# Leaving out 38 TensorE transposes of the identity ahead of the first gate product

## Chip, cores and metric

The kernel runs on one core of a Trainium2 chip. The metric is the device time of one execution in microseconds (us). The time of before is the median of three executions. One more execution was profiled; all rows below are from it. Engines: PE is TensorE, with its weight loads (PEld) recorded apart from its matmuls; DVE is VectorE, ACT ScalarE, POOL GpSimd, SP SyncE.

## The reference, cut to what matters

Two layers on `x` of shape (4, 256, 256): four batches `b`, 256 tokens, 256 channels. Each layer first makes its input by a bidirectional recurrence over tokens, gated by `sigmoid(x)`, and feeds it to a feed-forward part, whose output is added to `x`:

```python
x = x + _L0_ffn_ref(_L0_cond_ref(x, F, F, L0_w, L0_u, cond), A, Bw, Wg)
x = x + _L1_ffn_ref(_L1_cond_ref(x, F, F, L1_w, L1_u, cond), w1, b1, w2, b2)

def _bi_wkv(r, k, v, w, u, time_emb):      # both cond parts
    a = a * decay + exp(k) * v             # forward scan: num; with exp(k) alone: den
    ...                                    # the same backward
    return sigmoid(r) * (num / den) * (0.8 + 0.2 * tf)

def _L0_ffn_ref(x, A, Bw, Wg):             # top-1 mixture of 8 experts, rank 64
    prob = softmax(x @ Wg.T); gate = argmax(prob)
    h = einsum('nd,erd->ner', x, A) * one_hot(gate)
    return einsum('ner,eor->no', h, Bw) * 4 * prob[gate]

def _L1_ffn_ref(x, w1, b1, w2, b2):        # 256 -> 1024 -> 256, gelu, ternary weights
    return gelu(x @ q(w1).T + b1) @ q(w2).T + b2
```

The transposes that the change leaves out write a part of PSUM that nothing reads. They are no part of what is computed.

## The kernel before, in words

Channels lie on the 128 partitions (two halves `c`), tokens on the free axis, so that VectorE can do each recurrence as a scan along tokens. All engines have their instructions written out by hand, in one list for each, and wait for each other only by semaphores. TensorE's list is strictly in order: a wait in it holds back all that is listed behind it.

The work goes layer by layer and batch by batch, interleaved. For a batch of the first layer: VectorE scans forward (L708) and backward (L726), numerator and denominator; ScalarE takes logarithm and exponential for a reciprocal; VectorE or GpSimd multiply; `ratio` on VectorE (L738) ends this and raises `ratio_ready`. Then TensorE makes the gate product `gate_logits` (L1023: 8 columns, eight matmul records, each with the load of a 128x128 f32 weight) and the two halves of the first expert product, `expert_in` (L1038, sixteen records of 256 columns). VectorE reads the logits (`gate`, L743 to L755), makes the mask of the chosen expert (`expert_mask`, L768), TensorE transposes it (`transpose_mask`, L1045), ScalarE copies it out of PSUM (`copy_mask`, L473), VectorE multiplies it into the expert product (`select_expert`, L776), and TensorE makes the second expert product (`expert_out`, L1054). After that come tanh and the second layer, whose two products are `hidden` (L1101) and `ffn_out` (L1134).

The change touches TensorE's list alone. What stands in it just ahead of the gate product of batch 0 is `place_residual` (L1009), then `weight_totals` (L1062), which waits for ScalarE's sum over the second weight matrix (L497), and then five calls of `keep_warm`. Each waits for `AT_ready` and for one step of VectorE's (or GpSimd's) work on the first ratios, and then transposes the 128x128 identity `ident` (made at the start, and constant) into bank 7, 6, 8, 8, 8 and 8 times: 38 transposes (L939). The steps are the forward and backward numerator scans of batches 0 and 1, and `dr_ready[0]`, raised by `den_times_rec` (L236) just ahead of `ratio(0, 0)`. Bank 7 held a transposed half of A, which `AT_ready` says has been copied out. `warm_up(8)`, at the very start of the list (L933), stays.

After the gate product of batch 0 the list goes on:

```python
            gate_logits(0)
            expert_in(0, 0)
            expert_in(0, 1)
            transpose_mask(0)
            transpose_weights(0)
            gate_logits(1)
            expert_in(1, 1)
            expert_out(0)
```

VectorE's list at this place is `ratio(0, 0)`, `thresholds` (L781, L783), `backward(0, 2, DEN)`, `gate(0)`, `gate_index(0)`, `own_keys(0, 3)`, `times_sigmoid(1)`, `expert_mask(0)`, `ratio(0, 1)`, `own_values(0, 2)` (L216), `select_expert(0, 1)`, `select_expert(0, 0)`, `gate(1)`. ScalarE's is `sign_below(0)`, `gate_exp(0)`, `sign_above(0)`, `copy_mask(0)`, `sign_above(1)`.

Of the kernel before, what the change touches and what calls it, by code (L numbers as in the profile page):

```python
# [14 lines left out]
P = 128  # L15
# [8 lines left out]
def adaln_ffn_kernel(nc, x, fside, cond, w_l0, u_l0, A, Bw, Wg, w_l1, u_l1, w1, b1, w2, b2, out):  # L24
# [6 lines left out]
    NE, R, _ = A.shape  # L31
# [14 lines left out]
    with ExitStack() as ctx:  # L46
        def sb(name, shape, dt=F32, where=ctx):
            return where.enter_context(nc.sbuf_tensor(name, shape, dt))

        def sem(name):  # L50
            return ctx.enter_context(nc.semaphore(name))

        bank = [ctx.enter_context(nc.psum_tensor(f"bank{k}", [P, 512], F32)) for k in range(8)]

        ident = sb("ident", [P, P])
# [72 lines left out]
        def per(kind, n):  # L128
            return [sem(f"{kind}_{k}") for k in range(n)]
# [16 lines left out]
        fwd_done, seeded, bwd_done = [[per(f"{kind}{q}", RING) for q in ("num", "den")] for kind in ("fwd_", "seed_", "bwd_")]  # L146
        den_ready, num_ready = per("den_ready", RING), per("num_ready", RING)
        ln_done, rec_ready = per("ln_done", RING), per("rec_ready", RING)
        dr_ready, q_ready, ratio_ready = per("dr_ready", RING), per("q_ready", RING), per("ratio_ready", RING)
        qsig_ready = per("qsig_ready", NB)  # L150
        Wg_psum, A_psum, B_psum = sem("Wg_psum"), sem("A_psum"), sem("B_psum")
        WgT_ready, AT_ready, BT_ready = sem("WgT_ready"), sem("AT_ready"), sem("BT_ready")
# [18 lines left out]
        COND_BANK, DECAY_BANK, WARM_BANK, WT_BANK, MISC_BANK = 4, 5, 7, 4, 6  # L171
# [7 lines left out]
        NUM, DEN = 0, 1  # L179
# [748 lines left out]
        def _(pe):  # L928
# [3 lines left out]
                for _ in range(n):  # L932
                    pe.transpose(bank[WARM_BANK][:, 0:P], ident[:, :], ident[:, :])  # L933

            def keep_warm(done, count, n):
                pe.wait_ge(AT_ready, 2)
                pe.wait_ge(done, count)
                for _ in range(n):
                    pe.transpose(bank[WARM_BANK][:, 0:P], ident[:, :], ident[:, :])  # L939

            def transpose_vectors():
                pe.wait_ge(vec_loaded, 16 * 4)
                pe.transpose(bank[MISC_BANK][:, VEC_AT:VEC_AT + NV], vec_rows[:, :], ident[0:NV, 0:NV]).then_inc(vec_psum, 1)
# [68 lines left out]
            def gate_logits(b):  # L1012
                r, u = ring(0, b)
                pe.wait_ge(ratio_ready[r], u + 1)
                if b == 0:
                    pe.wait_ge(WgT_ready, 2)
                else:
                    pe.wait_ge(logits_ready, b)
                    pe.wait_ge(mask_copied, b)
                for n in range(NT):  # L1020
                    at = LOGIT_AT + NE * n
                    for c in range(NC):
                        mm = pe.matmul(bank[MISC_BANK][:, at:at + NE], nd[:, r, c, NUM, n * P:(n + 1) * P], WgT[:, c],  # L1023
                                       start=(c == 0), stop=(c == NC - 1))
                mm.then_inc(logits_psum, 1)
# [32 lines left out]
            def weight_totals():  # L1058
                pe.wait_ge(wsum_ready, 2)
                pe.wait_ge(consts_ready, 3)  # L1060
                pe.wait_ge(BT_ready, 2)
                pe.matmul(bank[WT_BANK][:, 0:2], ones[:, :], wsum[:, :], start=True, stop=True).then_inc(wtot_psum, 1)  # L1062
# [95 lines left out]
            place_residual(0)  # L1158
            place_residual(1)
            weight_totals()  # L1160
            keep_warm(fwd_done[NUM][0], 2, 6)
            keep_warm(bwd_done[NUM][0], 2, 8)
            keep_warm(fwd_done[NUM][1], 2, 8)
            keep_warm(bwd_done[NUM][1], 2, 8)
            keep_warm(dr_ready[0], 1, 8)
            gate_logits(0)
            expert_in(0, 0)
            expert_in(0, 1)
# [104 lines left out]
```

## Time and profile before

| | |
|---|---|
| median of three executions | 126.23 us (126.23, 126.23, 126.68) |
| profiled execution, its own time | 126.34 us |
| its span, first to last instruction | 124.5 us |
| around the span | 1.84 us |
| granted TensorE clock, mean over the span | 0.918 |
| busy share of the span | PE 81%, PEld 75%, DVE 87%, ACT 67%, POOL 42% |

Matmul and weight-load records overlap each other, so a group's busy time is less than its count times its mean duration; the pace of a group is read from the starts of its records. In the view by windows each column after the window and its length is an engine's busy time in it, with the number of records in brackets.

### The profile page before, as it was taken

What the parts mean: (1) busy time and instruction counts of PE and PEld (TensorE: products, weight loads), DVE (VectorE), ACT (ScalarE), POOL (GpSimd) and SP (SyncE); (2) the same over time, 40 slices, a digit from 0 to 9 for tenths busy, and PEclk for the clock granted to TensorE, in tenths of its full rate; (3) what the DMA queues carried; (4) which work ended last, traced back from release to release, by engine and by line L of the source; (5) the groups of instructions that cost most, each with busy time, mean ns of one, the idle gap of its engine ahead of it and who ended that gap; (6) DMA issues with size and microseconds to landing.
All of it is one profiled execution on the core that took longest, in us unless ns stands there. A gap on an engine that the chain in (4) does not pass through costs nothing.

```text
span 124.5 us, 2082 instructions
## 1 busy us (share of the span) xinstructions
PE 101.1 (81%) x654; PEld 93.7 (75%) x654; DVE 108.2 (87%) x218; ACT 83.0 (67%) x148; POOL 51.7 (42%) x61
## 2 busy tenths in 40 slices
PE   5596791099987999699725999967989799989991
PEld 5485790099976889599524899956979799989990
DVE  1389999999999999999999997999999999994731
ACT  4186989940676934469248549878099996997441
POOL 3077484817071149095703528409440390000530
PEclk9999689756999599999985599999999999999999
DMA  3899990000000000000000000000000002020004
GB/s 91 278 311 304 309 382 13 0 8 0 0 0 0 0 0 3 5 3 0 0 0 3 0 0 0 5 0 0 0 0 5 0 0 84 0 87 5 0 3 168
DMA packets 7271, 6.44 MB, mean 52 GB/s; under 512 B 2370, under 2 KB 7004, under 8 KB 7260
## 3 DMA queue, kind: packets, MB, share of 16 engines
q1 hardware_dynamic: 7244, 6.31, 16.3%
q8 instruction: 5, 0.08, 0.3%
q14 instruction: 6, 0.05, 0.1%
q10 hardware_dynamic: 16, 0.00, 0.0%
HBM read 5.26 MB, written 1.05 MB: 51 GB/s over the span
## 4 chain that ended last, share of the span: by engine, by line
DVE 58%; PE 17%; issue 17%; DMA 2%; DVEq 1%; ACT 1%; ACTq 0%
DVE run L708 14%; DVE nd L726 11%; PE bank L1134 6%; DVE own L695 4%; PE bank L1054 4%; DVE hm L776 4%; DVE mask L768 3%; PE bank L1101 3%; DVE nd L738 3%; DVE run L716 2%; DMA vec_rows<-in_L_cond_u_dram 2%; DVE nd L250 2%; DVE h_lo L262 2%; DVE nd L236 2%; DVE nd L223 2%
## 5 line engine op out<-in xcount | busy, mean ns | idle before, releaser
L708 DVE TENSOR_TENSOR_SCAN run<-bank,kv 128x256 f32<-128x256 f32 x32 | 20.1, 669 | 0.4
L726 DVE TENSOR_TENSOR_SCAN nd<-bank,run 128x256 f32<-128x256 f32 x32 | 20.1, 673 | 0.2
L1054 PE MATMUL bank<-hm,BT 128*128 128x256 f32 x64 | 16.9, 423 | 1.5 <-DVE hm L776 1.5
L1038 PE MATMUL bank<-nd,AT 128*128 128x256 f32 x64 | 17.7, 431 | 0.0
L1101 PE MATMUL bank<-xin_hi,w1T 128*128 128x256 f32 x64 | 15.8, 287 | 1.7 <-ACT h L536 1.2
L1054 PEld LDWEIGHTS bank<-hm,BT 128*128 128x128 f32 x64 | 13.6, 217 | 4.2 <-DVE hm L776 1.9
L262 POOL TENSOR_TENSOR h_lo<-h,h_hi 128x512 fp32r<-128x512 f32 x6 | 8.1, 1348 | 20.4 <-DVE h_hi L270 14.0
L1134 PE MATMUL bank<-w2T,h_hi 128*128 128x256 f32 x64 | 15.9, 287 | 0.5 <-DVE h_lo L262 0.5
L1038 PEld LDWEIGHTS bank<-nd,AT 128*128 128x128 f32 x64 | 15.8, 330 | 0.4
L1134 PE MATMUL bank<-w2T,h_lo 128*128 128x256 f32 x64 | 15.3, 278 | 0.0
L1101 PE MATMUL bank<-xin_lo,w1T 128*128 128x256 f32 x64 | 15.2, 279 | 0.0
L536 ACT ACTIVATE h<-bank,bT 128x256 f32<-128x256 f32 x32 | 12.9, 474 | 2.8 <-PE bank L1101 2.8
L1101 PEld LDWEIGHTS bank<-xin_hi,w1T 128*128 128x128 f32 x64 | 12.1, 189 | 2.2 <-issue 1.6
L1134 PEld LDWEIGHTS bank<-w2T,h_hi 128*128 128x128 f32 x64 | 12.0, 188 | 0.8 <-DVE h_lo L262 0.7
L216 POOL TENSOR_TENSOR own<-own,vs 128x512 f32<-128x512 f32 x6 | 8.2, 1361 | 9.9 <-DVE own L695 7.8
L1101 PEld LDWEIGHTS bank<-xin_lo,w1T 128*128 128x128 f32 x64 | 12.1, 189 | 0.0
L1134 PEld LDWEIGHTS bank<-w2T,h_lo 128*128 128x128 f32 x64 | 12.0, 188 | 0.0
L236 POOL TENSOR_TENSOR nd<-nd,run 128x512 f32<-128x512 f32 x5 | 6.4, 1272 | 12.2 <-ACT run L457 12.2
L230 POOL TENSOR_TENSOR nd<-nd,own 128x512 f32<-128x512 f32 x5 | 6.7, 1335 | 9.7 <-DVE nd L726 9.7
L262 DVE TENSOR_TENSOR h_lo<-h,h_hi 128x512 fp32r<-128x512 f32 x10 | 8.0, 796 | 2.0 <-ACT h_hi L269 1.9
L452 ACT ACTIVATE run<-nd 128x512 f32<-128x512 f32 x8 | 5.0, 623 | 6.1 <-DVE nd L223 6.1
L716 DVE TENSOR_TENSOR run<-run,inv_gain 128x2 f32<-128x2 f32 x16 | 7.6, 477 | 1.0
(131 smaller groups left out, 236.5 us busy)
## 6 DMA issues: line engine op xcount, KB each, us to landing
w_nat<-in_L_ffn_w_dram SPq DMA_DIRECT2D x2, 1024.0 KB, 8.1
F_nat<-in_fside_BxSxS_dram SPq DMA_DIRECT2D x4, 256.0 KB, 4.1
x_nat<-in_x_dram SPq DMA_DIRECT2D x4, 256.0 KB, 5.0
out_dram<-outb SPq DMA_DIRECT2D x3, 256.0 KB, 2.1
A_nat<-in_L_ffn_A_dram SPq DMA_DIRECT2D x1, 512.0 KB, 5.7
B_nat<-in_L_ffn_Bw_dram SPq DMA_DIRECT2D x2, 256.0 KB, 6.7
out_dram<-outb SPq DMA_DIRECT2D x2, 128.0 KB, 1.7
vec_rows<-in_L_cond_w_dram ACTq DMA_DIRECT2D x2, 1.0 KB
```

What stands on the lines that cost most here:

```text
L216: eng.tensor_tensor(own[:, r, :, NUM, :], own[:, r, :, DEN, :], vs[:, b], ALU.mult).then_inc(ownv_ready[r], 1)
L230: eng.tensor_tensor(num, num, own[:, r, :, NUM, :], ALU.add).then_inc(num_ready[r], 1)
L236: eng.tensor_tensor(den, den, run[:, r, :, DEN, :], ALU.mult).then_inc(dr_ready[r], 1)
L262: eng.tensor_tensor(h_lo[:, b % 2, 2 * j:2 * j + 2], h32[:, 2 * j:2 * j + 2], h_hi[:, b % 2, 2 * j:2 * j + 2].bitcast(F32), ALU.subtract). ...
L536: act.activation(h32[:, f], bank[g_bank[NJ * b + j]][:, (f % 2) * T:(f % 2 + 1) * T], ACT.Gelu, bias=bT[:, f:f + 1], scale=0.5).then_inc(h ...
L708: dve.tensor_tensor_scan(run[:, r, c, q], decay_ps[:, l, c, b:b + 1].broadcast_to([P, T]), kv[:, b, c, q], 0.0, ALU.mult, ALU.add).then_in ...
L716: dve.tensor_tensor(last, last, inv_gain[:, l, :, b], ALU.mult).then_inc(seeded[q][r], 1)
L726: dve.tensor_tensor_scan(nd[:, r, c, q, ::-1], decay_ps[:, l, c, b:b + 1].broadcast_to([P, T]), run[:, r, c, q, ::-1], 0.0, ALU.mult, ALU. ...
L1038: mm = pe.matmul(bank[H_BANK + k][:, (m % 2) * T:(m % 2 + 1) * T], AT[:, c, m::NM], nd[:, r, c, NUM, :], start=(c == 0), stop=(c == NC - 1))
L1054: mm = pe.matmul(bank[y_bank[b % 2]][:, o * T:(o + 1) * T], BT[:, m, o * P:(o + 1) * P], hm[:, b % 2, m], start=False, stop=(o == NC - 1 a ...
L1101: mm = pe.matmul(bank[g_bank[g]][:, (f % 2) * T:(f % 2 + 1) * T], w1T[:, c, f * P:(f + 1) * P], part[:, b % 2, c], start=(c == 0 and part ...
L1134: mm = pe.matmul(o_region(b, n), part[:, b % 2, f, n * P:(n + 1) * P], w2T[:, f], start=False, stop=(f == NF - 1 and part is h_lo and (n = ...
```

## The change

`keep_warm` and its five calls are taken out: 38 transposes on TensorE, with the waits ahead of them. No other engine's list changes, and no wait of any other instruction names anything that these transposes signal, for they signal nothing.

```diff
-            def keep_warm(done, count, n):
-                pe.wait_ge(AT_ready, 2)
-                pe.wait_ge(done, count)
-                for _ in range(n):
-                    pe.transpose(bank[WARM_BANK][:, 0:P], ident[:, :], ident[:, :])
-
...
             place_residual(0)
             place_residual(1)
             weight_totals()
-            keep_warm(fwd_done[NUM][0], 2, 6)
-            keep_warm(bwd_done[NUM][0], 2, 8)
-            keep_warm(fwd_done[NUM][1], 2, 8)
-            keep_warm(bwd_done[NUM][1], 2, 8)
-            keep_warm(dr_ready[0], 1, 8)
             gate_logits(0)
             expert_in(0, 0)
             expert_in(0, 1)
```

## Rows read from the trace of the kernel before

**Rows 1.** The page: the granted clock in 40 slices, and the chain by engine
```profile
PEclk9999689756999599999985599999999999999999
...
DVE 58%; PE 17%; issue 17%; DMA 2%; DVEq 1%; ACT 1%; ACTq 0%
```

**Rows 2.** Timeline of the weight loads: start us, length us, line, tiles, count, idle before
```profile
24.89 0.50 PEld L1062 LDWEIGHTS bank<-wsum,ones 128*128 128x128 f32 x2 [6.05 <-ACT h L497]
25.13 6.78 PEld L939 LDWEIGHTS bank<-ident 128*128 128x128 f32 x38
31.88 0.97 PEld L1023 LDWEIGHTS bank<-WgT,nd 128*128 128x128 f32 x8
32.77 3.83 PEld L1038 LDWEIGHTS bank<-nd,AT 128*128 128x128 f32 x16
38.08 0.20 PEld L1045 LDWEIGHTS bank<-ident,mask 128*128 128x128 f32 x2 [1.48 <-DVE mask L768]
```

**Rows 3.** Windows: length, busy PE, PEld, DVE, ACT, POOL, granted clock, DMA
```profile
16.50:17.00 0.50, 0.50 (x6) 0.50 (x5) 0.40 (x2) 0.25 (x1) 0.50 (x2) 0.74 1.05 416
...
19.03:23.58 4.55, 0.00 (x0) 0.00 (x0) 4.47 (x10) 4.51 (x7) 2.55 (x3) 1.00 0.00 1
23.58:24.89 1.31, 0.00 (x0) 0.00 (x0) 1.31 (x2) 1.26 (x2) 1.26 (x1) 0.50 0.00 0
25.34:30.41 5.07, 5.07 (x25) 5.07 (x26) 4.97 (x7) 1.35 (x2) 3.00 (x2) 0.50 0.01 3
30.41:31.88 1.47, 1.47 (x16) 1.47 (x14) 1.32 (x4) 0.00 (x0) 0.01 (x1) 1.00 0.00 0
40.65:44.06 3.41, 3.41 (x10) 2.71 (x10) 3.21 (x13) 3.17 (x9) 1.01 (x1) 0.50 0.00 0
67.88:71.37 3.49, 3.49 (x8) 2.86 (x9) 3.28 (x7) 2.36 (x3) 1.41 (x2) 0.50 0.00 0
```

**Rows 4.** Timeline of VectorE around the first gate
```profile
31.08 0.69 DVE L738 SCALAR_TENSOR_TENSOR nd<-nd 128x512 f32<-128x512 f32 x1
31.95 1.26 DVE L726 TENSOR_TENSOR_SCAN nd<-bank,run 128x256 f32<-128x256 f32 x2
33.13 0.15 DVE L743 COPY logits<-bank 128x16 f32<-128x16 f32 x1
35.80 2.23 DVE L768 TENSOR_SCALAR mask<-expert_of,idx,grec 128x128 f32<-128x128 f32 x2
39.15 1.28 DVE L776 TENSOR_TENSOR hm<-bank,mask_rows 128x512 f32<-128x512 f32 x2
```

**Rows 5.** Timeline of PE: weight totals and the first gate product
```profile
24.89 0.59 PE L1062 MATMUL bank<-wsum,ones 128*128 128x2 f32 x2 [5.86 <-ACT h L497]
31.99 0.96 PE L1023 MATMUL bank<-WgT,nd 128*128 128x8 f32 x8
```

**Rows 6.** Timeline of PEld: A's and B's transposes; `expert_out(2)` at each clock
```profile
13.16 0.59 PEld L969 LDWEIGHTS bank<-ident,x_nat 128*128 128x128 f32 x4 [1.97 <-issue]
13.74 1.72 PEld L986 LDWEIGHTS bank<-ident,A_nat 128*128 128x128 f32 x8
15.44 1.61 PEld L995 LDWEIGHTS bank<-ident,B_nat 128*128 128x128 f32 x8
68.05 0.76 PEld L1054 LDWEIGHTS bank<-hm,BT 128*128 128x128 f32 x2
70.60 0.76 PEld L1054 LDWEIGHTS bank<-hm,BT 128*128 128x128 f32 x2
```

**Rows 7.** Timeline of ScalarE: the mask's copy
```profile
38.56 0.38 ACT L473 ACTIVATE mask_rows<-bank 128x256 f32<-128x256 f32 x1 [2.01 <-PE bank L1045]
```

**Rows 8.** Timeline of PE and VectorE, 57 to 76 us: waits around `expert_out(2)`
```profile
57.97 3.67 PE L1054 MATMUL bank<-hm,BT 128*128 128x256 f32 x16
67.88 5.43 PE L1054 MATMUL bank<-hm,BT 128*128 128x256 f32 x16 [0.69 <-DVE hm L776]
75.53 0.17 DVE L743 COPY logits<-bank 128x16 f32<-128x16 f32 x1 [0.55 <-PE bank L1023]
```

## The prediction

> **What bounds the kernel now.** I read the page first: the chain that ended last is VectorE for 58% of the span, TensorE for 17% [rows 1]. The removed transposes lie in a stretch where VectorE is the chain, so they matter in two ways only: if the gate product had to queue behind them, and by what they do to TensorE's clock, which the slices show at half speed in four places [rows 1].
>
> The timeline of weight loads comes next [rows 2]. TensorE sat idle for 6.05 us until ScalarE's sum released `weight_totals` at 24.89. All 38 transposes then ran without a gap from 25.13 to 31.88, because most of their waits were over before they began. The gate product's loads started at 31.88, with the last transpose's load just ended. `ratio(0, 0)` ended at 31.08 + 0.69 = 31.77 [rows 4]. So the gate product followed its true releaser by 0.11 us.
>
> The windows show the clock [rows 3]. It was at 1.2 GHz (0.50) from 23.58, after 4.55 us without one TensorE record, through the first 25 transposes, and rose to 2.4 GHz (1.00) at 30.41, with nothing but transposes and the two small products of `weight_totals` behind it. The gate product and the first expert product ran at 2.4 GHz. TensorE then waited for VectorE: the mask's loads sat idle for 1.48 us before 38.08 [rows 2].
>
> **What the change does, step by step.**
>
> *The place in the queue.* The gate product's first load can start as soon as `ratio(0, 0)` releases it. The mask ended at 35.80 + 2.23 = 38.03 and its transpose's load began at 38.08 [rows 2, 4]: 0.05 us from end to start. So the load comes at 31.82 instead of 31.88 and 0.05 us (rounded down) is gained. Nothing else waited for the transposes.
>
> *The clock when the gate product starts.* TensorE now has nothing from about 25.4 to 31.82, some 6.4 us. The clock is low at 25.4 already; after an idle stretch of 4.55 us it was taken away, not given [rows 3]. So it stays at 1.2 GHz at 31.82.
>
> *The gate product at 1.2 GHz.* It is bound by its loads of 128x128 f32 weights: eight from 31.88 to 32.77, 0.111 us each [rows 2]. Loads of the same shape at 1.2 GHz ran at (15.44 - 13.74) / 8 = 0.2125 us [rows 6]. So the eight take 1.70 us instead of 0.89, and the expert product's first load comes at 31.82 + 1.70 = 33.52. The last gate matmul ends behind that load's start: by 31.99 + 0.96 - 32.77 = 0.18 us before [rows 2, 5]; at 1.2 GHz by 24.89 + 0.59 - 25.13 = 0.35 us (`weight_totals`, the next load at 25.13) [rows 2, 5]. It ends at 33.87, and with 0.05 us to the release VectorE's copy starts at 33.92 instead of 33.13 [rows 4]. The wait was hidden before: VectorE came to the copy from its own scan (31.95 + 1.26) [rows 4]. Now it is bare, **+0.8 us** on VectorE's list, and nothing in that list can go ahead of it. What hangs on it moves along: `own_keys(0, 3)`, on which GpSimd waits, `gate_exp` on ScalarE, and the mask, now released at 38.08 + 0.8 = 38.9.
>
> *The first expert product.* Its sixteen loads took 3.83 us at 2.4 GHz, 0.24 each [rows 2]. At 1.2 GHz the same form (`expert_out(2)`) had seven starts, that is six steps, from 68.05 to 70.60: 0.425 us each [rows 6]. What counts is when the clock rises. From restart to rise it took 71.37 - 67.88 = 3.5 us, 16.76 - 13.16 = 3.6 us (0.74 in the window 16.50:17.00 puts the rise at 16.76), and 30.41 - 24.89 = 5.5 us [rows 2, 3, 6]. From 31.82 these give 35.3 to 37.3; counted from the expert product at 33.52, since the gate product moves few columns, 37.0 to 39.0. I take 37.1, where the two readings meet. By then 8.4 loads have gone at 0.425; the other 7.6 take 1.8 us and end at 38.9. That is the moment when the mask is ready. So the 1.48 us in which TensorE waited is used up, and nothing is added. With a rise at 35.3 the mask is last, also nothing; with one at 39.0 the loads end at 33.52 + 12.9 x 0.425 + 3.1 x 0.24 = 39.75; with none, at 33.52 + 16 x 0.425 = 40.3. The mask's copy ended at 38.56 + 0.38 = 38.94 and its reader began at 39.15 [rows 4, 7], so 0.2 us more is free. The delay there is 0.8 us for an early or middle rise, 39.75 - 38.08 - 0.2 = 1.5 us for a late one and 2.2 us for none. I take 0.8, and keep 1.5 for the range.
>
> *Up to about 68 us.* TensorE's low stretch from 40.65 to 44.06 [rows 3] may go, as TensorE no longer idles just before it. I cost that at nothing: VectorE is the chain there, and its next wait for TensorE is at 75.53 [rows 8]. So the 0.8 us is carried on.
>
> *From 68 to 76 us.* `expert_out(2)` is on the chain, took 5.43 us (3.67 for `expert_out(1)` at 2.4 GHz) and was at 1.2 GHz until 71.37 [rows 3, 8]. Starting 0.8 us later, it gains nothing if the rise also comes 0.8 us later, and 0.8 x (1 - 0.24 / 0.425) = 0.35 us if it stays at 71.37, because less of it is then slow. The three distances from restart to rise differ by 2 us, so the trace favours neither end: I take the middle, **-0.15 us**. More than 0.55 us can't come back here, since VectorE waited just that long for TensorE [rows 8].
>
> **Sum**, against the profiled execution: 126.34 + 0.8 - 0.15 = 127.0 us (the queue's 0.05 is in the 0.8). It stood 0.11 above the median, which gives 126.9.
>
> **The rivals.**
>
> *The clock returns late.* The gate product may not count toward the rise and the next rise come 5.5 us after 33.52, or not before the expert product ends: delay 1.5 to 2.2 us, 127.6 to 128.3. For it: the 5.5 us of the restart at 24.89. Against it: dense products brought the clock back in 3.5 us at 67.88 [rows 3].
>
> *Not slower: the debt is paid back at `expert_out(2)`.* Its place is 67.88 to 75.53. Run wholly at 2.4 GHz it would be 5.43 - 3.67 = 1.76 us shorter, of which the 0.55 us that VectorE waits are on the chain. The time is 126.23 + 0.8 - 0.55 = 126.5, no change that can be told. It decides once the rise comes at least 0.55 / (1 - 0.24 / 0.425) = 1.3 us earlier, counted from the product's start, than the 3.49 us of before, or if the clock never falls near 64 us, because the preceding product, now 0.8 us later, fills what was idle. For it: that stretch moves toward the fall. Against it: TensorE still has a gap there of several us, with a few bf16 products in it.
>
> *The transposes do nothing for the clock.* Then before's rise at 30.41 had another cause, the gate product runs at 2.4 GHz in either kernel, and the 0.05 us is all: 126.2. Against it stands the rise itself [rows 3]. The Trainium skill ("TensorE: Matmul & The Clock Gate", part 4, on transposes by TensorE) says that full clock "doesn't engage" for transposes, as they don't count as busy in the same way; by that page the change would cost nothing. The trace disagrees: 38 transposes lay behind the change at 30.41.
>
> *Faster by over 0.5%.* For this the delay must stay away and the clock be higher at `expert_out(2)` as well; 126.23 - 0.05 - 0.55 = 125.6.
>
> **How the numbers follow.** 0.5% (0.63 us, a bound at 126.86) is about what a measurement of this kernel can tell from no change; its three executions spread by 0.45. Forecast 0.58: within it the delay at the end lies between 0.45 and 0.9 us, 126.6 to 127.1, with 0.37 of it above the bound and 0.21 below. Late clock 0.14, slower. Paid back 0.17, same. No effect 0.06, same. Faster 0.05. So slower 0.51, same 0.44, faster 0.05. For the range I leave out what lies below 126.3 (most of no effect, and faster) and the upper half of the late clock: 126.3 to 127.8.
>
> **What would show it right or wrong.** Right: no TensorE record between about 25.5 and 31.8; granted clock 0.50 there and through the gate product; its loads 0.21 us apart; VectorE's copy of the logits at about 33.9 with a wait of about 0.7 us for TensorE ahead of it; the mask's loads idle for almost nothing; the same distances between VectorE's steps from there to 68 us. Wrong: a granted clock of 1.00 at 31.9 (then the rule on transposes holds); a rise later than 38 us and a second wait of VectorE at its multiplication by the mask; a VectorE wait at the fourth gate's copy well away from 0.55 us; or a last-ended chain that no longer goes through VectorE between 33 and 68 us.

## The result and the profile after

Over nine executions each, the changed kernel took 127.77 us (127.14 to 128.44) and the kernel before 126.41 us (126.23 to 126.81): ratio 1.0108, 95% interval 1.008 to 1.0136. It is slower by about 1.4 us. The forecast of 126.9 had the sign and half of the size; the measured time lies 0.03 us inside the upper end of its range, 127.8. Ratios, here and below, are over the executions within 1.5% of the fastest of their kernel and medians over all, and where almost none lies that near the fastest only the median is given.

The profiled execution took 127.68 us, its span 125.8.

From here on, times inside an execution are also given from the start of `ratio(0, 0)`, since the first small loads land earlier or later by up to half a microsecond from one execution to the next and move all that follows; a plus sign marks such a time. That start is 31.08 before [rows 4] and 30.52 after.

The page of the changed kernel, clock in 40 slices and chain by engine:

```profile
PEclk9999689755569999968997569999999999999999
...
DVE 50%; PE 28%; issue 14%; ACT 2%; DMA 2%; DVEq 1%; ACTq 0%
```

TensorE's share of the chain rose from 17% [rows 1] to 28%, though it has 38 transposes less. The half-speed slices lie elsewhere: on through 31 to 37 us, a new place near 54 to 58, and near 68 to 75. The chain went through TensorE's gate product and first expert product from 31.27 to 38.8, where before it was VectorE's, and then, behind the copy of the mask, through VectorE up to the multiplications by the mask of batch 2 at 67.9.

Timeline of its weight loads, first gate to first mask (the lines are six lower than before):

```profile
31.27 1.78 PEld L1017 LDWEIGHTS bank<-WgT,nd 128*128 128x128 f32 x8 [6.34 <-DVE nd L738]
32.93 5.58 PEld L1032 LDWEIGHTS bank<-nd,AT 128*128 128x128 f32 x16
38.42 0.38 PEld L1039 LDWEIGHTS bank<-ident,mask 128*128 128x128 f32 x2
```

Timeline of its VectorE, at the same places as [rows 4, 8], and the mask of batch 2:

```profile
30.52 0.69 DVE L738 SCALAR_TENSOR_TENSOR nd<-nd 128x512 f32<-128x512 f32 x1
...
33.19 0.17 DVE L743 COPY logits<-bank 128x16 f32<-128x16 f32 x1 [0.53 <-PE bank L1017]
...
35.87 2.23 DVE L768 TENSOR_SCALAR mask<-expert_of,idx,grec 128x128 f32<-128x128 f32 x2
...
39.55 1.29 DVE L776 TENSOR_TENSOR hm<-bank,mask_rows 128x512 f32<-128x512 f32 x2 [0.25 <-ACT mask_rows L473]
...
61.28 2.66 DVE L768 TENSOR_SCALAR mask<-expert_of,idx,grec 128x128 f32<-128x128 f32 x2 [0.20 <-DVE grec L761]
...
77.82 0.17 DVE L743 COPY logits<-bank 128x16 f32<-128x16 f32 x1 [1.52 <-PE bank L1017]
```

The gate product's eight loads took 1.66 us (32.93 - 31.27) instead of 0.89. The copy of the logits came 2.67 us after `ratio(0, 0)` began, before 2.05: **0.62 us late**. The sixteen loads of the expert product took 5.5 us instead of 3.8 (38.42 - 32.93) and ended behind the mask (35.87 + 2.23 = 38.10), and the first multiplication by the mask began at +9.03 instead of +8.07: **0.96 us late**, with a wait for ScalarE's copy that was not there before. Then the delay was carried unchanged until the mask of batch 2, which took 2.66 us instead of 1.74. Windows show where the clock was (columns as in [rows 3]):

```profile
36.50:37.00 0.50, 0.50 (x3) 0.35 (x2) 0.50 (x2) 0.00 (x0) 0.50 (x2) 0.50 0.00 0
37.00:37.50 0.50, 0.50 (x4) 0.50 (x3) 0.50 (x1) 0.00 (x0) 0.50 (x1) 0.89 0.00 0
50.60:52.60 2.00, 0.15 (x3) 0.00 (x0) 2.00 (x5) 0.60 (x1) 0.00 (x0) 1.00 0.00 0
54.20:57.50 3.30, 3.30 (x8) 2.68 (x9) 3.20 (x11) 3.19 (x3) 2.88 (x3) 0.50 0.01 2
67.90:74.60 6.70, 5.73 (x17) 4.39 (x15) 6.39 (x11) 3.18 (x5) 2.53 (x3) 0.50 0.00 1
```

The rise came at 37.11 (0.89 of the window from 37.00). A new low stretch lies over the expert product of batch 2, at 54.2 to 57.5, some 1.5 us after the end of a pause of TensorE (0.15 us busy in 50.60 to 52.60).

How that reached VectorE is seen on ScalarE and GpSimd. The kernel before, timelines of the three engines at batch 2:

```profile
58.78 0.57 ACT L517 ACTIVATE w2T<-bank 128x512 fp32r<-128x512 f32 x1
59.26 0.70 ACT L457 ACTIVATE run<-run,recip_bias 128x512 f32<-128x512 f32 x1
...
60.04 1.27 POOL L236 TENSOR_TENSOR nd<-nd,run 128x512 f32<-128x512 f32 x1 [0.76 <-ACT run L457]
61.26 1.27 POOL L243 TENSOR_TENSOR nd<-nd,run 128x512 f32<-128x512 f32 x1
...
60.87 1.74 DVE L768 TENSOR_SCALAR mask<-expert_of,idx,grec 128x128 f32<-128x128 f32 x2 [0.21 <-DVE grec L761]
```

The changed kernel at the same place:

```profile
60.08 0.60 ACT L517 ACTIVATE w2T<-bank 128x512 fp32r<-128x512 f32 x1 [0.80 <-PE bank L1073]
60.58 0.71 ACT L457 ACTIVATE run<-run,recip_bias 128x512 f32<-128x512 f32 x1
...
61.37 1.27 POOL L236 TENSOR_TENSOR nd<-nd,run 128x512 f32<-128x512 f32 x1 [1.67 <-ACT run L457]
62.59 1.26 POOL L243 TENSOR_TENSOR nd<-nd,run 128x512 f32<-128x512 f32 x1
```

The slow expert product made TensorE's weight transposes behind it late. ScalarE waited 0.80 us for them in `evacuate_wT(4)`, which copies them out of PSUM (L517). `reciprocal(1, 0)` (L457) stood behind it in ScalarE's list, and so GpSimd's two products that need the reciprocal (the pair, L236 and L243) came 0.92 us later against the start of the mask's instructions (61.37 - 61.28 against 60.04 - 60.87). VectorE's second mask instruction ended only when that pair had: mask end 63.94, pair end 63.85 (before: 62.61 and 62.53). Where the pair misses them, the two instructions take 0.60 us. So the mask lost 0.92 us more than before. `expert_out(2)` was at 1.2 GHz almost throughout and VectorE waited 1.52 us at the fourth gate (that of batch 3) instead of 0.55; of the 2.85 us that it was late there, 1.2 were given back by the next mask (82.49, +51.97, before 81.37, +50.29), since two of VectorE's small steps no longer met GpSimd. At VectorE's last copy it stood at +92.65 against +90.82: 1.83 us late, about as much as the 0.96 at the first multiplication and the 0.92 at this mask together.

### The profile page after: what moved, and what is told of

It reads as the page before. It is cut to its first block, busy times and chain, and to the rows that moved or that the text cites. A ratio compares the mean times of both kernels' runs of the same rounds, so it can differ in the third digit from the quotient of the medians.

```text
span 125.8 us, 2001 instructions
## 1 busy us (share of the span) xinstructions
PE 97.9 (78%) x616; PEld 89.6 (71%) x616; DVE 108.0 (86%) x218; ACT 83.0 (66%) x148; POOL 51.8 (41%) x61
## 4 chain that ended last, share of the span: by engine, by line
DVE 50%; PE 28%; issue 14%; ACT 2%; DMA 2%; DVEq 1%; ACTq 0%
DVE run L708 12%; DVE nd L726 10%; PE bank L1032 8%; PE bank L1128 6%; PE bank L1048 5%; PE bank L1095 4%; DVE own L695 4%; DVE hm L776 4%; DVE nd L738 3%; DVE mask L768 2%; DVE run L716 2%; PE bank L1017 2%; DMA vec_rows<-in_L_cond_u_dram 2%; DVE h_lo L262 2%; DVE nd L236 2%
## 5 line engine op out<-in xcount | busy, mean ns | idle before, releaser
L1032 PE MATMUL bank<-nd,AT 128*128 128x256 f32 x64 | 19.7, 470 | 0.0
L1048 PE MATMUL bank<-hm,BT 128*128 128x256 f32 x64 | 17.4, 433 | 1.2 <-DVE hm L776 1.2
L1032 PEld LDWEIGHTS bank<-nd,AT 128*128 128x128 f32 x64 | 17.1, 330 | 1.5
L236 POOL TENSOR_TENSOR nd<-nd,run 128x512 f32<-128x512 f32 x5 | 6.3, 1270 | 14.6 <-ACT run L457 14.6
L1017 PE MATMUL bank<-WgT,nd 128*128 128x8 f32 x32 | 5.0, 282 | 8.3 <-DVE nd L738 8.2
L1017 PEld LDWEIGHTS bank<-WgT,nd 128*128 128x128 f32 x32 | 4.7, 225 | 8.7 <-DVE nd L738 8.4
L509 ACT ACTIVATE below<-w_nat,thr 128x2048 bf16<-128x2048 f32 x2 | 4.0, 2002 | 7.6 <-DVE thr L783 4.7
```

The lines of the kernel that those rows point to most:

```text
L236: eng.tensor_tensor(den, den, run[:, r, :, DEN, :], ALU.mult).then_inc(dr_ready[r], 1)
L1032: mm = pe.matmul(bank[H_BANK + k][:, (m % 2) * T:(m % 2 + 1) * T], AT[:, c, m::NM], nd[:, r, c, NUM, :], start=(c == 0), stop=(c == NC - 1))
L1048: mm = pe.matmul(bank[y_bank[b % 2]][:, o * T:(o + 1) * T], BT[:, m, o * P:(o + 1) * P], hm[:, b % 2, m], start=False, stop=(o == NC - 1 a ...
```

## The experiments

Ratios are against the kernel before on the same chip. "Before" had a median of 126.5 to 126.6 us in these calls and spread from 125.1 to 127.7 over more executions than were seen at first.

**The delay alone, at full clock** (`late_gate`; the kernel before, edited; `fill(n)` is n transposes of `ident` into bank 7 without a wait):

```diff
+            pe.wait_ge(ratio_ready[0], 1)
+            fill(7)
             gate_logits(0)
```

> The kernel before, with seven more transposes of the identity put between the end of ratio(0, 0) and the first gate product: at 2.4 GHz they hold it back by 7 x 0.116 = 0.8 us, about the delay that the changed kernel had, but the clock is high all through the first gate and expert product. Theory 1 (the change costs through the delay of the first gate and mask, and then through more low-clock stretches at batch 2 that the delay alone does not bring): 127.0 to 127.2 us, VectorE's copy of the first logits about 0.7 us later, no low clock between 31 and 39 us and none at 54 to 58 us. Theory 2 (the delay of VectorE is all, and the rest follows from it): the changed kernel's 127.8 us. Theory 3 (a delay there is absorbed further on): 126.4 us.

Median 127.13 us (125.77 to 128.31, twelve executions) beside 126.56 for before; ratio 1.0012 (0.9977 to 1.0048), which is without the three longest. The mean over all twelve is 126.99 against 126.43. In the profiled execution the copy of the logits stood at +2.56, about where the changed kernel had it, the clock was up from 29.06 to 52.96 and then low to 59.78, and the fourth gate came without a wait. The last copy was at +91.07. Of 0.51 us at the gate 0.25 was left at the end. The low stretch at 53 to 60, which I had expected to be absent, cost nothing here: GpSimd's pair, at 62.62, missed the mask (0.60 us) and met a later step. So theory 2 falls: neither the median nor this execution reaches 127.8. The median is in theory 1's range, but its condition of a high clock at 54 to 58 us was not met. The delay alone costs between nothing and about 0.6 us by these numbers.

**Keeping the clock up at batch 2** (`after_fill50`; the changed kernel, edited):

```diff
             transpose_weights(2)
+            fill(14)
             gate_logits(2)
```

> The changed kernel, with 14 transposes of the identity in TensorE's idle time ahead of the gate product of batch 2 (about 51 to 52.6 us). Theory 1 (the low clock at 54 to 58 us is a cost of its own: it makes ScalarE's reciprocal and GpSimd's products late, which then hold up VectorE's mask of batch 2 by 0.9 us): clock 1.00 there, that mask at 1.7 us instead of 2.66, and 0.3 to 0.9 us off, 126.9 to 127.5 us. Theory 2 (what is lost there is given back by 82 us anyway): 127.8 us.

Median 126.60 us; ratio 1.0032 (0.9999 to 1.0065), with a mean over all executions of 126.89 against 127.86 for the changed kernel. Theory 1 holds, and more went than I expected of it (its range ended at 126.9). Timelines of GpSimd and VectorE:

```profile
60.40 1.26 POOL L236 TENSOR_TENSOR nd<-nd,run 128x512 f32<-128x512 f32 x1 [0.76 <-ACT run L457]
...
61.23 1.74 DVE L768 TENSOR_SCALAR mask<-expert_of,idx,grec 128x128 f32<-128x128 f32 x2 [0.20 <-DVE grec L761]
...
76.84 0.17 DVE L743 COPY logits<-bank 128x16 f32<-128x16 f32 x1 [1.51 <-PE bank L1021]
```

No low clock between 36.1 and 66.8 us, the pair and the mask as before, and still 1.51 us of waiting at the fourth gate. That wait is thus no large part of the loss. Two things stand against reading the whole gain as that of batch 2: in this execution the clock rose at 36.12, a microsecond earlier than in the first of the changed kernel, so the first multiplication stood at +8.70 and not +9.03; and the same 14 transposes were not tried on the kernel before.

**Keeping it up at `expert_out(2)`** (`after_fill63`, and `before_fill63` on the kernel before):

```diff
             transpose_weights(5)
+            fill(18)
             transpose_weights(6)
+            fill(7)
             expert_out(2)
```

> The changed kernel, with 18 and 7 transposes of the identity in TensorE's idle time ahead of expert_out(2) (63 to 68 us). Theory 1 (that product at 1.2 GHz is what VectorE waits 1.5 us for at the fourth gate): expert_out(2) takes about 3.7 us instead of 6.4, the wait goes, 0.4 to 1.2 us off, 126.6 to 127.4 us. Theory 2 (given back by 82 us anyway, since 1.2 of the lead was): 127.8 us.

> The kernel before, with the same 18 and 7 transposes ahead of expert_out(2). expert_out(2) takes 3.7 us instead of 5.43 and VectorE's wait of 0.55 us at the fourth gate goes. Theory 1: 0.2 to 0.5 us off, 125.9 to 126.2 us. Theory 2 (VectorE's next contended steps take the gain back): 126.4 us.

On the changed kernel: median 127.60 us beside 126.56 for before. On the kernel before: median 126.37, ratio 1.0004 (0.9967 to 1.004). In both profiled executions `expert_out(2)` was short (3.72 and 3.62 us) and VectorE's wait at the fourth gate was gone, and yet neither median reached its theory 1's range (126.6 to 127.4, and 125.9 to 126.2). The first lies between that range and theory 2 (127.8), the second at theory 2 (126.4): what is gained there is mostly taken back.

**The changed kernel again, and eight transposes** (`after_again` is the changed kernel; `keep_last8` the kernel before with only its last call of `keep_warm`):

```diff
-            keep_warm(fwd_done[NUM][0], 2, 6)
-            keep_warm(bwd_done[NUM][0], 2, 8)
-            keep_warm(fwd_done[NUM][1], 2, 8)
-            keep_warm(bwd_done[NUM][1], 2, 8)
             keep_warm(dr_ready[0], 1, 8)
```

> The changed kernel once more, so that it stands beside the next ones on the same chip. Theory 1 and 2: 1.0 to 1.4 us slower than before, 127.5 to 127.9 us. Theory 3 (it lay in the chip or the hour): within 0.5 us of before.

> The kernel before with only the last eight of the 38 transposes (those behind dr_ready). They begin at about 29.3 us and take 1.7 us at 1.2 GHz. Theory A (what counts is how long TensorE has worked without a pause when the gate product comes): the clock is still 0.50 at the gate product and at the first half of the expert product, but rises up to 2 us earlier than in the changed kernel: 127.0 to 127.7 us. Theory B (a few transposes right ahead are enough): granted clock 1.00 at the gate product, 126.5 us. Theory C (they change nothing): as the changed kernel, 127.8 us.

The changed kernel: 128.14 us, 0.2 above the range expected, ratio 1.0133 (1.0089 to 1.0176), so the loss did not lie in the chip or the hour. Eight transposes: 128.16 us (one of the twelve took 135.19), ratio 1.0119 (1.0083 to 1.0155). Theory C: they change nothing in the time. Timeline of PEld of the second:

```profile
28.76 1.57 PEld L939 LDWEIGHTS bank<-ident 128*128 128x128 f32 x8 [4.94 <-issue]
31.17 1.78 PEld L1023 LDWEIGHTS bank<-WgT,nd 128*128 128x128 f32 x8 [0.84 <-DVE nd L738]
32.83 6.49 PEld L1038 LDWEIGHTS bank<-nd,AT 128*128 128x128 f32 x16
```

and the step where the late clock shows, in `after_again`'s timeline of VectorE:

```profile
40.67 1.29 DVE L776 TENSOR_TENSOR hm<-bank,mask_rows 128x512 f32<-128x512 f32 x2 [1.02 <-ACT mask_rows L473]
```

The clock rose at 39.02 with the eight transposes and at 39.16 in `after_again`, against 37.11 in the first execution of the changed kernel. That multiplication stood at +9.94 and +9.80, against +9.03 and, before, +8.07. With the other executions without the transposes (rise at 36.12, +8.70; 36.39, +8.71; 37.01, +8.85; 37.78, +9.20) the delay at the first multiplication runs from 0.6 to 1.9 us by where the rise falls.

The execution with eight transposes also shows that the loss can be made without the detour at batch 2. Its clock was up from 39.02 to 66.32, and its mask of batch 2 took 1.74 us, as before:

```profile
62.10 1.74 DVE L768 TENSOR_SCALAR mask<-expert_of,idx,grec 128x128 f32<-128x128 f32 x2 [0.21 <-DVE grec L761]
```

Yet its last copy stood at +92.95, 2.13 us late, of which 1.87 was there at the first multiplication by the mask.

**Taking ScalarE's reciprocal out from behind TensorE** (`after_swap`, `before_swap`):

```diff
             log_den(1, 0)
-            evacuate_wT(4)
             reciprocal(1, 0)
+            evacuate_wT(4)
```

> The changed kernel with ScalarE's reciprocal(1, 0) moved ahead of its copy evacuate_wT(4), so that the reciprocal no longer waits for TensorE's products of batch 2. Theory 1 (half of the loss is made at 61 us: the low clock there makes that copy late, with it the reciprocal and GpSimd's two products, which then stand in the way of VectorE's mask): the reciprocal ends by 60 us whatever the clock, GpSimd's pair starts at about 60 us instead of 61.4, the mask's two instructions take 1.7 us or less instead of 2.66, and 0.5 to 0.9 us go: 126.9 to 127.3 us. Theory 2 (the lost time is given back later anyway): 127.8 us.

> The kernel before with the same swap. In its profiled execution the reciprocal did not wait, so theory 1 says: no change there, but fewer long executions, where the clock happens to be low at 54 to 58 us; median 126.3 to 126.6 us. Rival: GpSimd's pair now always falls on VectorE's mask, where in some executions it fell on the later seed step: slower by up to 0.3 us.

The changed kernel with it: median 126.85 us, against 126.50 for before. The kernel before with it: 126.27, ratio 0.9983 (0.995 to 1.0017), no change, as its theory says. ScalarE and GpSimd in `after_swap`, with the clock low from 54.07 to 57.48 all the same:

```profile
59.51 0.72 ACT L457 ACTIVATE run<-run,recip_bias 128x512 f32<-128x512 f32 x1
60.14 0.58 ACT L517 ACTIVATE w2T<-bank 128x512 fp32r<-128x512 f32 x1
...
60.31 1.27 POOL L236 TENSOR_TENSOR nd<-nd,run 128x512 f32<-128x512 f32 x1 [0.51 <-ACT run L457]
```

and VectorE's mask there:

```profile
61.38 1.55 DVE L768 TENSOR_SCALAR mask<-expert_of,idx,grec 128x128 f32<-128x128 f32 x2 [0.20 <-DVE grec L761]
```

This edit leaves the clock as it is and cuts only the path by which it reached VectorE, and about 0.9 us or more went (127.77 and 128.14 to 126.85). It is about the amount that went with the clock kept up (127.77 to 126.60). Theory 1 holds by two independent ways, and for this one the same edit on the kernel before gave nothing.

**What is left without the detour** (`before_swap_fill`, `after_swap_fill`: the swap and the 25 transposes ahead of `expert_out(2)`, on each kernel):

> The kernel before with the reciprocal of batch (1, 0) ahead of the copy and with the 25 transposes ahead of expert_out(2). Theory: both later places where the clock touches VectorE's chain are off it; 0.2 to 0.6 us below before, 125.9 to 126.3 us. Rival: VectorE and GpSimd collide elsewhere instead, 126.5 us.

> The changed kernel with the same two edits, so that only what it loses up to VectorE's first multiplication by the mask is left. Theory: that delay is 0.6 us from the gate product, and up to 1.9 us where the clock rises late; against the kernel before with the same edits it is 0.6 to 1.2 us slower, 126.6 to 127.3 us. Rival (most of the change's price was made further on): within 0.4 us of the kernel before with the same edits.

126.55 us, ratio 1.0029 (0.9996 to 1.0062), and 127.02 us, ratio 1.0064 (1.0039 to 1.009). The second is 0.47 us above the first; with the swap alone the two differ by 126.85 - 126.27 = 0.58 us. The theory's difference (0.6 to 1.2) was too high and the rival's (within 0.4) too low, and the two kernels' intervals overlap, so this difference is the likeliest size, not a proven one. The first expectation failed: both edits together bring the kernel before nothing.

**Fewer transposes** (`keep_first30`: without the last call; `keep30_swap_fill`: that with the other two edits):

```diff
             keep_warm(bwd_done[NUM][1], 2, 8)
-            keep_warm(dr_ready[0], 1, 8)
             gate_logits(0)
```

> The kernel before without the last eight transposes only (30 of 38 stay). Where the clock rises late, the 38 take up to 38 x 0.213 = 8.1 us from 25.1 us and hold the gate product back themselves; 30 take at most 6.4 us and end by 31.5, ahead of the release. Theory (the transposes are worth their clock and cost their place in the queue): clock up by the gate product or at most one or two us later, its first load no later than 0.1 us behind ratio(0, 0), median 0 to 0.3 us below before, 126.2 to 126.5 us. Rival (the pause that is left makes the clock fall or stay low): 127.0 us or more.

> All that helped, together: 30 transposes ahead of the first gate product, the reciprocal ahead of the copy, 25 transposes ahead of expert_out(2). Theory: the fastest of all, 125.6 to 126.1 us. Rival: no better than the kernel before, 126.5 us, since VectorE is busy throughout and collides with GpSimd elsewhere.

The reason for the first lay in `before_swap`, where the 38 transposes themselves were late. Timelines of PE and VectorE of that kernel:

```profile
24.97 7.12 PE L939 MATMUL bank<-ident 128*128 128x128 f32 x38
31.92 0.96 PE L1023 MATMUL bank<-WgT,nd 128*128 128x8 f32 x8
...
30.42 0.69 DVE L738 SCALAR_TENSOR_TENSOR nd<-nd 128x512 f32<-128x512 f32 x1
...
32.92 0.17 DVE L743 COPY logits<-bank 128x16 f32<-128x16 f32 x1 [0.36 <-PE bank L1023]
```

`ratio(0, 0)` ended at 31.11 and the gate product started 0.8 us later, behind the transposes: copy at +2.50, almost as late as the +2.66 without any. With 30 of them: median 125.81 us (expected 126.2 to 126.5), ratio 0.9948 (0.9916 to 0.9979), the only kernel whose interval lies below before. The gain must be read with care: the ratio is without its two longest executions, 127.12 and 127.75 us, and the mean over all twelve is 126.11 against 126.39. Its profiled execution was one of these two (127.12 us). Timeline of PE there:

```profile
24.95 5.94 PE L939 MATMUL bank<-ident 128*128 128x128 f32 x30
31.73 1.06 PE L1023 MATMUL bank<-WgT,nd 128*128 128x8 f32 x8 [0.85 <-DVE nd L738]
32.65 5.61 PE L1038 MATMUL bank<-nd,AT 128*128 128x256 f32 x16
```

The gate product was in time and at full clock (copy at +2.06); the clock fell at 33.42, after the 0.85 us pause, and the expert product ran slow, but the mask still began its multiplication at +8.08. The loss was made at batch 2 again (mask 2.66 us). The last combination, 126.44 us and 0.9981 (0.9947 to 1.0014), is not the fastest: its theory falls and the rival (126.5) holds.

## Why the forecast had the sign and half of the size

*Place in the queue:* right for the profiled execution, where the gate product came 0.06 us behind `ratio(0, 0)` after and 0.11 before. But the cost that I set at 0.05 us is not a constant: in `before_swap` the gate product came 0.8 us behind `ratio(0, 0)`, and the copy 0.45 us later than before (+2.50 for +2.05).

*The clock at the gate product:* right. It stayed at 1.2 GHz from 23.5 to 37.1. The rival by which transposes do nothing for the clock is out: it rose behind nothing but them and the two small products of `weight_totals` in every execution with 30 or 38 that was profiled, at 28.3 to 30.7, and where they were left out or only eight stayed, it rose at 36.1 to 39.2.

*The gate product at 1.2 GHz:* the loads took 1.66 us for 1.70 forecast. The tail of the last product was 31.27 + 1.88 - 32.93 = 0.22 us, not 0.35, so VectorE was 0.62 late, not 0.8.

*The first expert product:* the loads ended 0.3 us behind the mask rather than with it: 0.96 us late instead of 0.8. That the rise fell at 37.11 for 37.1 forecast was luck. The forecast took three distances from restart to rise, 3.5 to 5.5 us; in the seven profiled executions without the transposes or with eight, the distance from the gate product's start was 4.6 to 7.9 us. In two of them the rival of the late clock was what happened, with 1.7 and 1.9 us late.

*Up to about 68 us: this step failed.* "I cost that at nothing: VectorE is the chain there, and its next wait for TensorE is at 75.53", and "so the 0.8 us is carried on". VectorE indeed waited for TensorE itself nowhere between, but TensorE reached it through ScalarE's list and GpSimd: the mask of batch 2 took 2.66 us for 1.74. The step looked only for direct waits. By the medians, what two experiments take away there is about 1 us of 1.4 to 1.6, and what stands without it is 0.5 to 0.6 by the two pairs of kernels with the swap. In single executions the parts differ: 0.96 us at the first multiplication and 0.92 at the mask of batch 2 in the first of the changed kernel, 1.73 and 0.91 in `after_again`, 1.87 and nothing with eight transposes.

*From 68 to 76 us:* I forecast that 0.15 us would come back; 0.97 more were waited (1.52 for 0.55, which the forecast named as a sign of being wrong), and 1.2 were given back by 82 us through steps that the forecast did not look at. Keeping the clock up there changed the kernel before by nothing measurable (1.0004).

The measured time is inside the range, but not for the reason of its upper end. That end stood for a late rise of the clock; in the profiled execution of 127.68 us the rise came when forecast, and the detour at batch 2, for which the range had no term, made up the rest.

The spread that the forecast called 0.45 us was that of three executions; in 35 it was 2.5 us. Why the low stretch at batch 2 comes in the changed kernel stays open. Its TensorE worked at full clock from 37 us, where before had a low stretch [rows 3], was done earlier and paused longer ahead of the gate product of batch 2 (1.92 us by the timeline of PE, before 0.43). But this pause does not decide it: `keep_last8` and `before_swap` paused 1.92 and 2.00 us there and had no low stretch, and `before_swap_fill` paused 0.59 us and was low from 53.29 to 56.70. In `late_gate` and `before_fill63` the stretch came and GpSimd's pair missed the mask. How often each case occurs in either kernel stays open too, as one or two executions of each were profiled.

## What to carry to other kernels

A matmul engine that is off the chain can still reach it through a third engine: list what stands in order behind each instruction that waits for it, and follow that to the products which share time with the chain's engine. Transposes in idle time can be worth their clock (without these 38 the kernel was 1.1 to 1.3% slower), but what waits behind them pays for their slow case. A count that ends before the release even at half clock, 30 here, was the fastest that was measured. Where the clock decides, profile several executions before pricing anything under one per cent.

## What the runs showed of the hardware that was not expected

Eight transposes with a pause of 0.84 us behind them did not bring the clock up any sooner than none (rise at 39.02, against 36.12 to 39.16 in the six executions with none). Two VectorE instructions that together take 0.60 us took 1.74 or 2.66 us when GpSimd's products of 1.27 us each ran beside them, so the same work cost up to 2.06 us more by when the other engine started. The Trainium skill ("SBUF — State Buffer", section "Who interferes with whom") has the port pair that VectorE and GpSimd share as an exclusive lock, which the other engine waits out in full. The trace of the changed kernel agrees as far as it goes, since the mask ended at 63.94, just behind the pair's end at 63.85; no run here took the port itself away.
